# A graph network on one core: the first convolution as a slot layer

## The chip, the cores and the metric

The kernel runs on one core of one Trainium2 chip. The metric is the device time of one execution in microseconds (us). The kernel before takes 2701.87 us (median of 3 runs, 2697.64 to 2702.93).

## What is computed

A graph has 3125 nodes with 128 features and 53125 edges, each with a source, a target, one of 8 types and 16 attributes. Four networks follow one another; each adds its result to x and normalizes:

```python
h = relu(x @ proj + b)                       # network 0, two rounds
for l in range(2):
    msgs = trans[edge_type, src]             # trans = h times edge_W[l][t], t of 8
    agg = segment_sum(msgs, dst)
    h = relu(gru_cell(agg, h))
x = layernorm(x + h @ out_w + out_b)
# network 1: three rounds of the same form, with messages divided by the count
# of their (type, target), root weights, a bias and a residual
# network 2: one aggregation to the source node, scaled by degrees
# network 3: mean of the edge attributes by target and by source, then an MLP
```

A network's sum over edges is called a convolution here. Network 0 has two of them, network 1 three, network 2 one.

## The kernel before

**Start (lines 517 to 536, 1042, 808, 1253, 1532).** SyncE loads biases, weights and x, then the edge lists. TensorE projects x to h in 7 chunks and multiplies each of 25 blocks of h by the 8 type weights. ScalarE and VectorE bring each product to `big`, SyncE writes it to a table `messages` in DRAM. VectorE's list arithmetic (`window_starts`, `rows`, `sender_blocks`) runs between these copies, then come `windows` and `edge_data`, which also write constants. The semaphore `zeros` says that these are done. SyncE then clears the attribute rows in DRAM and loads marks.

**First loop (`first_loop` on each engine).** The edges are taken in 52 groups of 8 tiles of 128. Per group, GpSimd gathers 8 tiles of messages from the table (line 694), TensorE adds them into the window of targets by one-hot products (834), VectorE adds that to `acc` (1590). This is the first convolution. The loop also builds what the later layers need: ranks of the edges within blocks of source nodes (TensorE 817 and 818, VectorE's `ranks`, line 1561 first), counts by target and type (842), and the placing of every edge's payload in a slot (ScalarE 1274, 1280, 1285, TensorE 848, adding into one PSUM bank). TensorE's order is: rank product of group g+1, then messages, counts and slots of group g. Marks (the edge attributes) have four buffers; SyncE reloads one when ScalarE has copied it (`attr_kept`).

**After the loop.** VectorE turns the bank into slot lists (`slots`, lines 1739 to 1759), counts cells (`count_cells`, to 1777) and places them (`place_cells`, 1781 to 1806), beside the first recurrent unit (`gru(0, i)`, 7 chunks; line 1993 is VectorE's first step in a chunk). Its state product (line 926) has run before the loop.

**Slot layers.** Every other convolution of networks 0 and 1 is one. A *tile* (125 of them): VectorE compares a list of slots with the lane number (`shot`, line 1902), TensorE spreads the rows of a source block over the slots (956), ScalarE copies the result to `xs` (1302), SyncE stores 256 KB of records in `chunks`. Tiles come in 5 rounds of 25. A *window* (149): GpSimd gathers 128 records of 2 KB by an index list (`rec`, line 694, 6 buffers), VectorE builds four one-hots of target and type (`dhot`, 1923), TensorE sums (984). After each 12 windows a *transform* multiplies the sums by the 8 type weights (969). `plan(k)` orders tiles and windows. Layer 1, the second convolution, does all tiles and then all windows; in layers 2, 3 and 4 (network 1) windows follow their tiles by a round and the layers run into one another (`joined`). A window may be gathered when the last tile of its round is stored.

In layer 1, GpSimd also puts a target code beside each record (751), and VectorE beside the tiles inverts the counts (from tile 20), judges flags (tile 60) and makes the index list in six pieces (`list_piece`, lines 1827 to 1835, from tile 66 on). `list_piece` needs two lists that SyncE stores and loads back (656, 658).

**Edge attributes.** GpSimd scatters every tile of them to a row by rank in DRAM (`send_attrs`, line 703, 416 scatters), for the last aggregation. They stand in GpSimd's order beside layer 1 (96), ahead of and beside layer 2 (128), beside layers 3 and 4 (88 each) and ahead of the last aggregation (16). Their marks are loaded again, into weight buffers that are free by then.

The order of all this is written out by hand: each engine runs its own list, and semaphores join them.

## Time and profile before

| What | us |
|---|---|
| Median of 3 runs | 2701.87 |
| The profiled execution | 2686.08 |
| Its span, first to last instruction | 2684.0 |
| TensorE busy in the span | 2390.2 |
| VectorE busy | 1844.6 |
| GpSimd busy | 1591.1 |
| ScalarE busy | 856.3 |
| Message table's products (lines 808, 809; 50 and 50) | 26.4 and 25.5 |
| Gathers of messages in the loop (416) | 400.0 |
| Gathers of records in layers 1 to 4 (596) | 589.4 |

The mean clock granted to TensorE was 0.964 of full speed. Busy time counts instructions at work; an engine that waits for a semaphore is idle. GpSimd's instructions for a transfer end before the transfer lands. A row of the timeline gives in brackets how long the engine was idle before it, and whose end it waited for.

### The profile page before, as it was taken

To read this page: it belongs to the slowest core of one execution; us is meant where nothing else is said; L and a number is where in the kernel's file an instruction comes from. 1 tells how busy PE (TensorE), PEld (TensorE's weight loads), DVE (VectorE), ACT (ScalarE), POOL (GpSimd) and SP (SyncE) were. 2 spreads that over 40 slices of the span, in tenths; PEclk is the share of its full clock that TensorE was granted. 3 is DMA by queue.
4 is the path that set the end of the run, shared out by engine and by line. 5 is a ranking of instruction groups with operands and counts; after the bars stand their busy time and mean duration, and the time that the engine had idled before them with its cause. 6 is when DMAs were issued, how large, how long until landed. Compare 5 with 4: busy or idle time off the path is not lost.

```text
span 2684.0 us, 45747 instructions
## 1 busy us (share of the span) xinstructions
PE 2390.2 (89%) x15645; PEld 2130.7 (79%) x15645; DVE 1844.6 (69%) x6137; ACT 856.3 (32%) x1498; POOL 1591.1 (59%) x1706
## 2 busy tenths in 40 slices
PE   7798888886877999879999989999899987987998
PEld 3587777773777998569999989999899985876896
DVE  4887777766775886687776588766567874443785
ACT  3476665652442111332222322212222210444002
POOL 0777777765566664755666367776377773677000
PEclk9899999998998999799999999999999997999999
DMA  8422222222997665179998799888899871677891
GB/s 299 125 65 63 61 63 62 63 51 92 252 253 212 181 172 147 32 225 280 281 276 257 249 294 287 260 265 253 276 282 271 261 203 39 213 261 240 262 268 55
DMA packets 271661, 520.15 MB, mean 194 GB/s; under 512 B 62015, under 2 KB 115698, under 8 KB 270645
## 3 DMA queue, kind: packets, MB, share of 16 engines
q1 hardware_dynamic: 185197, 289.49, 34.9%
q0 software_dynamic: 86224, 227.59, 29.3%
q8 instruction: 134, 2.20, 0.3%
q14 instruction: 106, 0.87, 0.1%
HBM read 323.93 MB, written 192.99 MB: 193 GB/s over the span
## 4 chain that ended last, share of the span: by engine, by line
PE 50%; POOL 20%; DMA 12%; issue 8%; DVE 7%; ACT 2%; DVEq 0%; SPq 0%; POOLq 0%; ACTq 0%
PE ps L984 21%; POOL msg L694 15%; PE ps L956 9%; PE ps L969 6%; PE ps L1199 5%; DMA rec<-chunks,idx 4%; DMA chunks<-xs 3%; DMA chunks<-xo,put_idx 2%; POOL chunks L792 2%; POOL rec L694 2%; DVE shot L1902 1%; PE ps L1174 1%; POOL attributes L703 1%; PE ps L1018 1%; DMA srow<-lanes_of_slots 1%
## 5 line engine op out<-in xcount | busy, mean ns | idle before, releaser
L694 POOL DMA_INDIRECT rec<-chunks,idx x596 | 589.4, 989 | 366.8 <-PE ps L984 142.6
L984 PE MATMUL ps<-dhot,rec 128*128 128x168 f32 x4768 | 739.4, 310 | 52.2 <-DMA rec<-chunks,idx 29.7
L984 PEld LDWEIGHTS ps<-dhot,rec 128*128 128x128 f32 x4768 | 694.8, 192 | 71.1 <-DVE dhot L1923 37.3
L1923 DVE TENSOR_SCALAR dhot<-iota,dcode 128x168 f32<-128x168 f32 x2384 | 589.1, 311 | 93.7 <-PE ps L984 85.5
L956 PE MATMUL ps<-hrow,shot 126*128 126x128 f32 x4000 | 498.7, 279 | 51.5 <-DVE shot L1902 39.6
L956 PEld LDWEIGHTS ps<-hrow,shot 126*128 126x128 f32 x4000 | 477.9, 194 | 64.0 <-issue 32.4
L694 POOL DMA_INDIRECT msg<-messages,idx_buf x416 | 400.0, 962 | 195.7 <-issue 195.4
L1302 ACT ACTIVATE xs<-ps 128x512 f32<-128x512 f32 x500 | 296.8, 597 | 668.4 <-PE ps L956 604.9
L703 POOL DMA_INDIRECT attributes<-w,rank_to x368 | 373.9, 1016 | 178.9 <-issue 119.1
L1902 DVE TENSOR_SCALAR shot<-srow,lane_no 126x512 f32<-126x512 uint8 x500 | 232.3, 490 | 89.7 <-DMA srow<-lanes_of_slots 50.1
L848 PE MATMUL ps<-big,lane1h 128*128 128x300 f32 x832 | 224.0, 423 | 0.7 <-ACT big L1285 0.7
L1965 DVE TENSOR_TENSOR agg_rows<-ps,tmp 128x504 f32<-128x504 f32 (+1 forms) x150 | 101.4, 676 | 157.0 <-PE ps L984 155.2
L848 PEld LDWEIGHTS ps<-big,lane1h 128*128 128x128 f32 x832 | 153.9, 190 | 55.4 <-issue 9.1
L792 POOL DMA_INDIRECT chunks<-xo,put_idx x149 | 147.1, 987 | 82.2 <-ACT xo L1409 49.2
L1280 ACT ACTIVATE tmp<-iota,slot_col 128x300 f32<-128x300 f32 x416 | 186.3, 530 | 10.5 <-DVE slot_col L1574 10.4
L1174 PE MATMUL ps<-yrows,thot 126*128 126x128 f32 (+1 forms) x1192 | 150.8, 285 | 31.3 <-ACT xo L1409 28.6
L969 PE MATMUL ps<-agg_rows,w 128*128 128x252 f32 (+1 forms) x832 | 178.6, 368 | 0.0
L1174 PEld LDWEIGHTS ps<-yrows,thot 126*128 126x128 f32 (+1 forms) x1192 | 142.6, 198 | 38.8 <-ACT xo L1409 35.5
L969 PEld LDWEIGHTS ps<-agg_rows,w 128*128 128x128 f32 x832 | 151.4, 190 | 15.1
L2118 DVE TENSOR_SCALAR thot<-trow,lane_no 126x512 f32<-126x512 uint8 x149 | 79.1, 532 | 109.3 <-PE ps L1174 108.7
L834 PE MATMUL ps<-onehot,msg 128*128 128x128 f32 x832 | 105.2, 280 | 52.9 <-DMA msg<-messages,idx_buf 52.9
L834 PEld LDWEIGHTS ps<-onehot,msg 128*128 128x128 f32 x832 | 98.6, 193 | 64.3 <-issue 64.3
(289 smaller groups left out, 2495.6 us busy)
## 6 DMA issues: line engine op xcount, KB each, us to landing
chunks<-xs SPq DMA_DIRECT2D x375, 256.0 KB
tmp<-inverse_counts SPq DMA_DIRECT2D x36, 1008.0 KB, 10.3
chunks<-xs SPq DMA_DIRECT2D x125, 258.0 KB
srow<-lanes_of_slots SPq DMA_DIRECT2D x100, 320.0 KB, 5.7
grec<-chunks SPq DMA_DIRECT2D x125, 256.0 KB
messages<-big SPq DMA_DIRECT2D x25, 504.0 KB
trow<-lanes_of_targets SPq DMA_DIRECT2D x30, 320.0 KB, 4.1
rec<-chunks,idx POOLq DMA_INDIRECT x596, 5.0
```

The source lines that it names most:

```text
L694: eng.indirect_dma_start(buf, None, table, bass.IndirectOffsetOnAxis(ap=index, axis=0)).then_inc(sem, 16)
L703: eng.indirect_dma_start(attr_d, bass.IndirectOffsetOnAxis(ap=rank_to[:, c:c + 1], axis=0), attr_rows(k, n // G)[:, n % G * TC + T:(n % G ...
L792: eng.indirect_dma_start(x1_d, bass.IndirectOffsetOnAxis(ap=put_idx[:, v:v + 1], axis=0), xo[:, v % XO, :], None)\
L834: last = mm(ps[:, g % 2, 0:P], msg[:, g % SUB, t, :], onehot[:, g % 2, t, :], start=t == 0, stop=t == G - 1)
L848: last = mm(ps[:, 7, near_col(g):near_col(g) + NEAR], lane1h[:, g % 2, t, :], big[:, g % 2, t * NEAR:(t + 1) * NEAR], start=False, stop=Fa ...
L956: last = mm(ps[:, STAGE1_BANKS[i % 3], j * P:(j + 1) * P], shot[0:BS, i % SS, j * P:(j + 1) * P], hrow[0:BS, sb_, :], start=True, stop=True)
L969: last = mm(out, wt(REL[k], T)[:, t * P:(t + 1) * P], agg[gi % 2][:, t, 0:c1 - c0], start=t == 0, stop=k == 1 and t == T - 1)
L984: last = mm(ps[:, 4 + i % 2, (v % 3) * WT:(v % 3 + 1) * WT], rec[:, v % RS, j * P:(j + 1) * P], dhot[:, v % DS, j * WT:(j + 1) * WT], star ...
L1174: last = mm(ps[:, STAGE1_BANKS[v % 3], j * P:(j + 1) * P], thot[0:nodes_of(c), v % SS, j * P:(j + 1) * P], yrows[0:nodes_of(c), c, :], sta ...
L1302: act(xs[:, i % XS, 0:4 * P], ps[:, STAGE1_BANKS[i % 3], :], ACT.Copy).then_inc(q("x1_evac"), 1)
L1902: vec.tensor_scalar(shot[0:BS, i % SS, :], srow[0:BS, s_ % NS, (n % QS) * SPAN:(n % QS + 1) * SPAN], lane_no1[0:BS], None, ALU.is_equal).t ...
L1923: last = vec.tensor_scalar(dhot[:, v % DS, j * WT:(j + 1) * WT], iota[:, 0:WT], dcode[:, v, j:j + 1], None, ALU.is_equal)
```

## The change

The first convolution leaves the loop: the message table, its stores, the gathers, the message products and the additions to `acc` go. It becomes slot layer 1. The former layers 1 to 4 become 2 to 5. Layers 1 and 2 are woven by the same `plan`: windows follow their tiles by a round, transforms between them.

The edge lists are loaded first, and the list arithmetic runs at once. The record rows in DRAM are cleared in 50 transfers during the loop. The first state product stands within layer 1, at tiles 64 to 100, on ScalarE's copies. `slots`, `count_cells` and `place_cells` stand before layer 1. In layer 1 the flags are judged at tile 5, the six list pieces come at tiles 8 to 18 and the inverse counts at tiles 26 to 50. ScalarE puts the target codes, not GpSimd.

The scatters of attributes are divided anew. Those of the 26 even groups go out in the loop, from the marks that are there; GpSimd computes their rows itself (nine small operations per group). Those of the 26 odd groups go out beside layers 1 and 2, 104 in each, 0.7 behind each window's gather. Layers 3 to 5 and the last aggregation have none.

```diff
-AT = {1: range(0, 12), 2: range(12, 28), 3: range(28, 39), 4: range(39, 50), 5: range(50, 52)}
...
+AT = {1: range(0, LATE_GROUPS // 2), 2: range(LATE_GROUPS // 2, LATE_GROUPS)}
...
+CLEARS = 50
+LISTED, INVERTED, STATES = 22, 56, range(64, 106, 6)
...
-                at.append((NQ + v if k == 1 else when, 1, "sums", v))
+                at.append((when, 1, "sums", v))
...
+        def woven(k):
+
+            for kind, n in plan(k):
+                yield kind, n
+                if kind == "sums" and n % GW == 4 and n >= GW:
+                    yield "transform", n // GW - 1
+            yield "transform", NGRP - 1
...
+            def first_layer():
+                for kind, i in woven(1):
+                    if kind != "tile":
+                        continue
+                    store_tile(1, i)
+                    if i == LISTED:
+                        eng.wait_ge(q("idx_ready"), PIECES)
+                        attr_load(1)
+                    if i == INVERTED:
+                        eng.wait_ge(q("inv_ready"), INV_PIECES)
+                        eng.dma_start(inv_d, res[TYPE_ROWS, 0:NU]).then_inc(q("inv_stored"), 16)
...
+                for s in range(NS - 1):
+                    lanes_load(2, s)
+                after(eng, "gru_h", 0, NCH)
+                attr_load(2)
...
-            table_stores(0, flat)
...
+            for g in range(NG):
+                eng.wait_ge(q("attr_kept"), g + 1)
+                if g % 2 == 0 and g >= SUB:
+                    marks_sent(eng, g - SUB)
+                eng.dma_start(mark[:, g % SUB, :], mark_d[:, ds(g * (G * TC), G * TC)])\
+                   .then_inc(q(f"mark_loaded_{g % SUB}"), 16)
+                if g < CLEARS:
+                    n = RECS // CLEARS
+                    eng.dma_start(x1_d[g * n:(g + 1) * n, :].rearrange("(p r) c -> p r c", r=5),
+                                  no_rows[0:n // 5].unsqueeze(1).to_broadcast([n // 5, 5, RECORD_COLS]))\
+                       .then_inc(q("records_cleared"), 16)
...
-            attr_load(attrs_0, AT[1][:6])
-            attr_load(attrs_2, AT[1][6:])
+            eng.wait_ge(q("rows_cleared"), 32)
+            eng.wait_ge(q("lanes_stored"), 16)
+            for s in range(NS - 1):
+                lanes_load(1, s)
...
-            layer(1)
+            eng.wait_ge(q("records_cleared"), 16 * CLEARS)
+            first_layer()
+            second_layer()
...
+            def rows_of_ranks(g):
+
+                tiles = slice(g * G, (g + 1) * G)
+                eng.wait_ge(q("slot_known"), g + 1)
+                st.did(eng.tensor_scalar(sent[:, 0, :], rank_f[:, tiles], float(CAP), 1e6, ALU.is_ge, ALU.mult))
+                st.did(eng.tensor_scalar(sent[:, 1, :], src_sb[:, tiles], float(CAP), None, ALU.mult))
+                st.settle()
+                st.do(eng.tensor_tensor(sent[:, 1, :], sent[:, 1, :], sent[:, 0, :], ALU.add))
+                st.do(eng.tensor_tensor(sent[:, 1, :], sent[:, 1, :], rank_f[:, tiles], ALU.add))
+                st.did(eng.tensor_scalar(sent[:, 0, :], sent[:, 1, :], float(RANKS), None, ALU.is_ge))
+                st.did(eng.tensor_tensor(sent[:, 2, :], own_row[:, tiles], sent[:, 1, :], ALU.subtract))
+                st.settle()
+                st.do(eng.tensor_tensor(sent[:, 2, :], sent[:, 2, :], sent[:, 0, :], ALU.mult))
+                st.do(eng.tensor_tensor(sent[:, 1, :], sent[:, 1, :], sent[:, 2, :], ALU.add))
+                st.do(eng.tensor_copy(rank_to[:, tiles], sent[:, 1, :]))
...
+            def send_marks(g):
+
+                s = g % SUB
+                eng.wait_ge(q(f"mark_loaded_{s}"), 16 * (g // SUB + 1))
+                for t in range(G):
+                    c = g * G + t
+                    eng.indirect_dma_start(attr_d, bass.IndirectOffsetOnAxis(ap=rank_to[:, c:c + 1], axis=0),
+                                           mark[:, s, t * TC + T:(t + 1) * TC], None).then_inc(q(f"mark_sent_{s}"), 16)
...
-            eng.wait_ge(q("code_ready"), 1)
-            eng.wait_ge(q("rows_cleared"), 32)
-            for n in range(AT_FIRST[1]):
-                send_attrs(1, n)
-            for i in range(NQ):
-                if i >= XS:
-                    slot_wait(eng, "x1_stored", XS, 1, NQ, i - XS)
...
-                if i % 2 == 0:
...
+            rows_of_ranks(0)
+            for g in range(0, NG, 2):
+                if g + 2 < NG:
+                    rows_of_ranks(g + 2)
+                send_marks(g)
             eng.wait_ge(q("idx_ready"), PIECES)
...
                     rows_of(rec[:, v % RS, :], x1_d[0:RECS + 1, :], idx[:, v:v + 1], q(f"rec_got_{v % RS}"))
-                    if k == 2 and v % 3 == 1 and AT_FIRST[k] + v // 3 < G * len(AT[k]):
-                        send_attrs(k, AT_FIRST[k] + v // 3)
-                    n = 2 * (v // 3 - 4) + v % 3 - 1
-                    if k >= 3 and v % 3 > 0 and 0 <= n < G * len(AT[k]):
-                        send_attrs(k, n)
...
+                    if k <= 2:
+                        n = G * len(AT[k])
+                        for i in range(v * n // NW, (v + 1) * n // NW):
+                            send_attrs(k, i)
...
+            def first_state(c):
+
+                if c >= 1:
+                    after(eng, "state_kept", 0, c)
+                mm(bank(3, c), wt("whh0_n"), chunk(h, c), start=True, stop=True).then_inc(q("state_mm"), 1)
...
             def first_layer():
-                for i in range(NQ):
-                    spread_slots(1, i)
-                for v in range(NW):
-                    sum_window(1, v)
-                    if v % GW == 4 and v >= GW:
-                        transform(1, v // GW - 1)
-                transform(1, NGRP - 1)
+                for kind, n in woven(1):
+                    if kind == "tile":
+                        if n in STATES:
+                            first_state(STATES.index(n))
+                        spread_slots(1, n)
+                    elif kind == "sums":
+                        sum_window(1, n)
+                    else:
+                        transform(1, n)
...
-            candidate_state(0)
             eng.wait_ge(q("far_known"), 1)
+            after(eng, "h_ready", 0, NCH)
             first_loop()
...
             eng.wait_ge(q("loop_done"), 1)
+            eng.wait_ge(q("loaded_rest"), 2 * 16)
+            for c in range(NCH):
+                turn_rows(1, c)
+            eng.wait_ge(q("src1_ready"), 1)
+            for j in range(4):
+                last = mm(ps[0:NQ, 7, j * P:(j + 1) * P], src1[:, j * NQ:(j + 1) * NQ], wt("ident"), start=True, stop=True)
+            last.then_inc(q("lanes_mm"), 1)
+            eng.wait_ge(q("lanes_ready"), 1)
+            eng.wait_ge(q("cells_known"), 1)
+            mm(ps[0:TB, 7, 0:NWP], wb("before", TB, TB), cells, start=True, stop=True).then_inc(q("starts_mm"), 1)
+            first_layer()
...
+                    turn_rows(2, i - 1)
...
-            candidate_state(1)
-            first_layer()
+            second_state()
+            second_layer()
...
+            def first_state(c):
+
+                if c == 0:
+                    eng.wait_ge(q("inv_stored"), 16)
+                after(eng, "state_mm", 0, c + 1)
+                act(chunk(res, c), bank(3, c), ACT.Copy).then_inc(q("state_kept"), 1)
...
             first_loop()
+            for c in range(NCH):
+                keep_rows(1, c)
+            layer(1)
+            attrs_sent(eng, 1)
             for i in range(NCH + 1):
                 gru(0, i)
                 if i >= 1:
-                    keep_rows(1, i - 1)
-            layer(1)
+                    keep_rows(2, i - 1)
+            layer(2)
+            attrs_sent(eng, 2)
...
+                st.do(vec.tensor_tensor(to, rank, own, ALU.min))
+                eng.wait_ge(q("pool_steps"), RANK_STEPS * (NG // 2))
...
                 eng.wait_ge(q("placed"), NG + 1)
+                eng.wait_ge(q("records_cleared"), 16 * CLEARS)
...
-                beside = {1: [(20 + 4 * a, invert_counts, a) for a in range(INV_PIECES)] + [(60, judge)]
-                             + [(66 + 4 * a, list_piece, a) for a in range(PIECES)]}.get(k, [])
+                beside = {1: [(5, judge)] + [(8 + 2 * a, list_piece, a) for a in range(PIECES)]
+                             + [(26 + 4 * a, invert_counts, a) for a in range(INV_PIECES)]}.get(k, [])
...
-            for c, beside in enumerate([window_starts, None, rows, None, sender_blocks] + [None] * (NCH - 5)):
-                table(0, c, flat)
-                if beside:
-                    beside()
+            window_starts()
+            rows()
+            sender_blocks()
             windows()
             edge_data()
-            keep_state(0)
...
             rank_rows()
             slots()
             count_cells()
+            place_cells()
+            layer(1)
             for i in range(NCH):
                 gru(0, i)
-                if i == 2:
-                    place_cells()
             keep_state(1)
-            layer(1)
+            layer(2)
```

## Rows read from the trace of the kernel before

**Rows 1.** The profile's page, parts 1 and 5: engines, and TensorE's message products.
```profile
PE 2390.2 (89%) x15645; PEld 2130.7 (79%) x15645; DVE 1844.6 (69%) x6137; ACT 856.3 (32%) x1498; POOL 1591.1 (59%) x1706
...
L834 PE MATMUL ps<-onehot,msg 128*128 128x128 f32 x832 | 105.2, 280 | 52.9 <-DMA msg<-messages,idx_buf 52.9
```

**Rows 2.** Timeline of one loop period: start us, us, engine line op, operands, [idle before <-releaser].
```profile
343.51 0.36 DVE L1561 TENSOR_TENSOR rank_prod<-sb1h,ps 128x200 f32<-128x200 f32 x1 [2.21 <-PE ps L818]
...
347.43 3.58 ACT L1280 ACTIVATE tmp<-iota,slot_col 128x300 f32<-128x300 f32 x8
...
348.68 0.94 POOL L694 DMA_INDIRECT msg<-messages,idx_buf  x1 [0.30 <-issue]
...
348.90 4.31 PE L848 MATMUL ps<-big,lane1h 128*128 128x300 f32 x16
...
351.05 2.30 ACT L1285 ACTIVATE big<-tmp,w 128x2400 f32<-128x2400 f32 x1
...
353.92 0.36 DVE L1561 TENSOR_TENSOR rank_prod<-sb1h,ps 128x200 f32<-128x200 f32 x1 [2.21 <-PE ps L818]
```

**Rows 3.** Windows, third layer: us, PE PEld DVE ACT POOL busy (x), clock, DMA, GB/s.
```profile
1660.00:1760.00 100.00, 97.22 (x696) 94.55 (x695) 72.05 (x242) 20.40 (x35) 76.57 (x77) 1.00 0.90 268
```

**Rows 4.** Timeline around the second recurrent unit and the next layer's start.
```profile
1067.35 1.11 PE L917 MATMUL ps<-acc,w 128*128 128x504 f32 x2 [1.48 <-issue]
...
1150.90 3.59 PE L956 MATMUL ps<-hrow,shot 126*128 126x128 f32 x24 [1.15 <-DVE shot L1902]
...
1194.56 1.11 POOL L694 DMA_INDIRECT rec<-chunks,idx  x1 [17.69 <-DMA chunks<-xs]
```

**Rows 5.** Timeline of the start: VectorE's last constant, ScalarE's first marks.
```profile
79.42 0.15 DVE L1501 TENSOR_SCALAR lane_no<-lane_no 128x1 f32<-128x1 f32 x1
...
96.96 0.31 ACT L1274 ACTIVATE marks<-mark 128x128 f32<-128x128 f32 x1 [16.55 <-DMA mark<-in_marks]
```

**Rows 6.** Groups by line: busy us, mean ns | idle before; the addition into acc.
```profile
L1590 DVE TENSOR_TENSOR acc<-acc,ps 128x128 f32 x52 | 14.4, 276 | 8.7 <-PE ps L834 8.7
```

**Rows 7.** Instructions on the tile code: duration ns min/median/max, first and last start.
```profile
L751 POOL COPY xs<-code x125: 176/193/857, 662.8 to 827.7; 128x4 f32<-128x4 f32 x125
```

**Rows 8.** Chain of waits (start us, us, what): the last attribute scatter's landing.
```profile
829.31 3.59 DMA attributes<-rec,rank_to
```

**Rows 9.** Transfers by issuing line: count, size, median us from issue to landing.
```profile
mark<-in_marks SPq DMA_DIRECT2D x52, 96.0 KB, 2.0
...
agg_rows<-lists SPq DMA_DIRECT2D x1, 1950.0 KB, 9.2
tmp<-lists SPq DMA_DIRECT2D x1, 1875.0 KB, 6.9
```

**Rows 10.** Timeline from the loop's last product to the end of the placing of cells.
```profile
602.67 4.31 PE L848 MATMUL ps<-big,lane1h 128*128 128x300 f32 x16
...
618.74 0.30 DVE L1777 TENSOR_TENSOR dhot<-dhot 25x150 f32<-25x150 f32 x1
...
638.77 0.30 DVE L1781 COPY dhot<-ps 25x150 f32<-25x150 f32 x1 [1.83 <-PE ps L1080]
...
642.33 0.72 DVE L1993 SCALAR_TENSOR_TENSOR tmp<-res,bias,tmp 128x504 f32<-128x504 f32 x1
```

**Rows 11.** Chain of waits: tiles (8 matmuls each), a transform (16), windows (8 each).
```profile
674.02 3.82 PE ps L956 x32
...
1265.65 3.40 PE ps L969 x16
1273.29 3.42 PE ps L984 x24
```

**Rows 12.** Timeline of VectorE: the starts of two pieces of the list.
```profile
754.71 0.55 DVE L1827 TENSOR_SCALAR dhot<-agg_rows,lane_no 128x650 f32<-128x650 f32 x1
...
761.14 0.55 DVE L1827 TENSOR_SCALAR dhot<-agg_rows,lane_no 128x650 f32<-128x650 f32 x1
```

**Rows 13.** Waits of TensorE in the fourth layer: us in total, times, longest us.
```profile
PE ps L984 <- DMA rec<-chunks,idx: 15.8, 14, 3.9
```

More of the change, by code:

```diff
@@ L43 @@
 PASSES = NG // SUB
-AHEAD = 3
 NONE = 8191
@@ L606, in layer @@
                         inv_load(i // GW + 1)
[L607 to L608 removed]
+                after(eng, "acc_evac", 5, NGRP)
+                for j in (3, 4, 5):
                     general(j)
@@ L761, in _ @@
+            for k in range(1, 6):
                 for v in range(NW):
-                    if k == 1 and v == 0:
-                        for i in range(NQ - XS, NQ):
-                            slot_wait(eng, "x1_stored", XS, k, NQ, i)
-                    if k >= 2 and v in (0,) + LIMITS:
+                    if v in (0,) + LIMITS:
                         done = TB * (((0,) + LIMITS).index(v) + 1)
-                        done = ROUND_0 if k >= 3 and v == 0 else done
+                        done = ROUND_0 if k >= 4 and v == 0 else done
@@ L969, in transform @@
                     last = mm(out, wt(REL[k], T)[:, t * P:(t + 1) * P], agg[gi % 2][:, t, 0:c1 - c0], start=t == 0,
-                              stop=k == 1 and t == T - 1)
-                if k >= 2:
-                    last = mm(out, wt(f"root{k - 2}"), feed(k)[:, c0:c1], start=False, stop=True)
+                              stop=k <= 2 and t == T - 1)
+                if k >= 3:
+                    last = mm(out, wt(f"root{k - 3}"), feed(k)[:, c0:c1], start=False, stop=True)
                 last.then_inc(q("xf_mm"), 1)
@@ L1336, in layer @@
                             keep_rows(j, n)
-                for j in (1,) if k == 1 else (2, 3, 4):
+                for j in (3, 4, 5) if k == 3 else (k,):
                     with bad(eng):
@@ L1951, in layer @@
                         update(j, n)
-                after(eng, "acc_evac", 4, NGRP)
-                for j in (2, 3, 4):
+                after(eng, "acc_evac", 5, NGRP)
+                for j in (3, 4, 5):
                     general(j)
```

505 lines of the change are left out of this document (208 added, 297 removed).

## The prediction

> **What bounds the kernel now.** I read the busy shares first, then the stages, then one period of the long loop, then the queue of GpSimd.
>
> TensorE is busy 2390 of 2684 us [rows 1], so 294 us of idling is all that a better order could win while its work stays. The first loop does not run at TensorE's pace. One of its 52 groups takes 353.92 - 343.51 = 10.4 us, and the row that closes it shows VectorE waiting 2.2 us for TensorE [rows 2]. TensorE is late because GpSimd issues one gather per 0.94 + 0.30 = 1.24 us, so 8 gathers take 9.9 us: GpSimd sets the pace. From the layers on, TensorE is nearly full: 97.2 of 100 us in the stretch of [rows 3], with GpSimd at 77 instructions in the same 100 us, one per 1.30 us. That is GpSimd's ceiling as well: 76.57 us of busy time over 77 is 0.99 each, and with the 0.30 us of issue that stands between any two [rows 2] the queue is full.
>
> **The change, part by part.** I build the new timeline from the span's start and compare it with that of before at one point: the first tile of the third aggregation (the second of before), at 1150.90 us [rows 4].
>
> *Start.* The table of messages and the first state product go, the list loads come first. Before, VectorE finishes its constants at 79.4 us and ScalarE's first copy of marks starts 17.5 us later, at 97.0, behind the clearing of the attribute rows in the DMA queue [rows 5]. Now VectorE starts as its lists land (near 8 us; about 1.1 MB), does the same lane arithmetic (about 25 us in all), and waits once for the projections, since the flag product stands behind them in TensorE's order. I put the constants at 38 us (33 if the projections are early, 42 if late) and ScalarE's start at 55.5, with 50 and 60 as bounds.
>
> *The loop.* 416 gathers, 832 matmuls and 52 additions leave it; 26 groups of 8 scatters come in, each led by nine small GpSimd operations, and 50 transfers that clear records. GpSimd then has (8 x 1.30 + nine operations) per two groups, about 14 us, and is no longer full. Two things can be late next. VectorE: its part of a period is 10.4 - 2.2 = 8.2 us, less the 0.28 us addition that goes [rows 6]; that leaves 7.9 at most, and about 7.4 if some half a microsecond of small waits within it goes too. And a new ring: the marks of an even group are reloaded only when GpSimd has sent the group four before, and it sends that one only after it has the ranks of the group two before. I walk once round. Nine small operations: the nearest row is GpSimd's copy of codes, 0.19 us at the median and 0.86 at most [rows 7]; with a wait behind most of them I take 3.5 us for the nine (2 to 8). Eight scatters: 7 x 1.30, and 3.6 from the last one's start to its landing [rows 8], 12.7. The reload of marks: 2.0 [rows 9], and 0.2 for SyncE. ScalarE: a copy of 0.3 [rows 5], then 351.05 + 2.30 - 347.43 = 5.9. TensorE's slot product and the rank product behind it, to VectorE's start: 353.92 - 348.90 = 5.0. VectorE to the next rank: between 2 and 3.9 (its start at 343.51 to ScalarE's at 347.43, which holds a wait); I take 2, since the ten operations there are short. Sum 31.6 us, and it spans four groups: 7.9 each. With the ring and VectorE this close I take 8.0 (7.4 to 9.1). SyncE stands in that wait too; behind it are the record clearings and the odd group's marks, which have several us to spare. The clearings (0.66 MB each, some 3 us) are hidden by a DMA system that has little else there.
>
> So the last slot product ends at 55.5 + 10 (the first group's way) + 51 x 8.0 = 473.5. Before, it ends at 602.67 + 4.31 = 607.0 [rows 10]. That is 133.5 us won.
>
> *Between loop and layer.* Before, the slot lists, the counts and the placing of cells run beside the first recurrent unit. Now the first tile waits for them. From 607.0 to the last count operation is 12.1 us, the placing is 642.33 - 638.77 = 3.6, the counting product between them about 0.6, and the first comparison and tile 1.3. I take 17.5; the transposes of the first chunks lie beside it. First tile at 491.
>
> *First convolution as a layer.* TensorE's work for it is new: per tile 3.82 / 4 = 0.955 us, per window 1.14, per transform 3.40 [rows 11], so 125, 149 and 13 of them are 119 + 170 + 44 = 333 us. But what ends last is GpSimd. Its 149 gathers and 104 scatters at 1.30 are 329 us, and none of it can start before the 25 tiles of the first round are stored and the list of chunks is there. That start is late here. The list loads take 9.2 and 6.9 us [rows 9] and are asked for once the placing is done, so they land some 18 us behind the first tile; VectorE comes to the first piece at tile 8 and stands there, with all shots behind it, and TensorE behind them. Six pieces follow at 6.4 us with four shots between [rows 12], so about 5.6 with two: 33 us. Then the tiles up to the 24th and their landing, and the load of attributes in the same queue. I take 63 us from the first tile to the first gather (55 to 75). To the end: 148 windows of 253 x 1.30 / 149 = 2.21 us are 327, then landing, one-hots, window, transform and evacuation, 13. Sum 403. The state products (7 x about 0.9) lie in TensorE's slack: 100 tiles, 149 windows and 13 transforms are 309 us or 2.08 per window, against GpSimd's 2.21; the inverse counts and codes lie in VectorE's.
>
> *First recurrent unit.* Before, 674.02 - 607.0 = 67 us from loop end to first tile. Its first VectorE step waited for the lists and counts (about 6 of their 12.1 us; the gates' products take the rest) and later for the placing (3.6): 57 without them.
>
> *Second convolution.* The same plan without lists. The like layer of before needs 1194.56 - 1150.90 = 43.7 us to its first gather, with a reduction beside each tile that these layers lack; I take 39. Then 327 + 13. Sum 379. Before, the layer took 1067.35 - 674.02 = 393 [rows 4, 11]: first all tiles, then all windows. The weaving wins 14 us and not the 50 that TensorE's work would allow, because the scatters put GpSimd in its place.
>
> *The rest.* The next two layers to carry scatters lose them. In the last of them TensorE waits 15.8 us for records [rows 13], and those waits are where scatters and a load of marks hold gathers up. I count 20 us for all three (5 to 35). The 16 scatters ahead of the last aggregation lie beside normalization and give nothing.
>
> **The sum.** First tile of the third aggregation: 491 + 403 + 57 + 379, and 83.5 for the second recurrent unit and its normalization (1150.90 - 1067.35), is 1413.5. That is 262.6 later than 1150.9; less 20, 243. The profiled execution took 2686.1 us (span 2684.0), so 2929 on its scale; the median of the three runs is 2701.9, 0.6% more, so I forecast 2945.
>
> In short, the way from loop end to that tile grows from 544 to 940 us, by 396, and the 416 gathers that go give back 133.5, since VectorE needs the loop for 7.4 us or more of each 10 anyway.
>
> **Rivals.**
> *1. TensorE's pace in the two new layers.* If gathers run far enough ahead, a window costs 2.08 or less instead of 2.21 and the tail is short: about 25 us less in each, 2895. Against it: in [rows 3] a lighter load (five instructions per three windows, 2.17 us) already keeps GpSimd full. For it: TensorE still reaches 97% there. 0.13.
> *2. A slow ring.* VectorE and GpSimd hold each other up, and the nine operations take 8 us instead of 3.5: 36 us round, 9.1 each, 57 us more, 3002. The codes' copy, four elements wide, goes from 0.19 to 0.86 us beside a VectorE less busy than in the loop [rows 7]. 0.2.
> The Trainium skill (SBUF — State Buffer, "SBUF: two separate sides") has a rule for it: VectorE with two inputs in SBUF, or in a two-port mode, and a GpSimd operation lock one port pair, each for its whole instruction. The trace agrees for the small copies by their 0.86 us; the gathers' 0.94 beside a busy VectorE show little of it.
> *3. Not slower.* TensorE's idling is all lack of gathered data, and the new order fills it. Its own work rises by 333 and falls by 105, the message products [rows 1], and by some 50 for the table: about 178 more. So it decides in favour if the 294 us of idling fall to 116 or less, to 4% of the span; at 116 it gives the 2702 of before. Against it: VectorE alone holds the loop to 7.4 us a group, and about 50 us of gaps are new (17.5 ahead of the layer, and of its first 63 us what 25 tiles of 0.955 leave over). 0.02.
> My forecast, with its own range of 2905 to 2980: 0.65.
>
> **How the numbers follow.** The likeliest case gives 2945. The range takes in its bounds (loop at 7.4: -31; a start 10 us off; 63 as 75) and most of rivals 1 and 2: 2882 to 3010. About 0.2% is what a measurement here can tell from no change. Slower 0.98, same 0.01, faster 0.01.
>
> **What would show it.** Right: a loop of 8 us per group with GpSimd idle in it; a gap of 17 to 18 us without tiles behind it; VectorE waiting near the eighth tile for the lists; and in the two new layers TensorE waiting for gathered records, with GpSimd at 77 instructions per 100 us. Wrong: a loop period over 8.5 (the ring), GpSimd waiting for windows in those layers (rival 1), or the transfers of records as the longest wait, which I left out because the new layers load no inverse counts.

## The result: 2916 us, 7.96% slower

The changed kernel takes 2916.47 us (median of 4 runs, 2911.35 to 2919.85) where the kernel before took 2701.94 beside it: a ratio of 1.0796, 95% interval 1.0775 to 1.0816. The forecast was 2945 with a range of 2882 to 3010. The profiled execution took 2914.79 us, its span is 2912.9. A second set on another chip gave 2910.17 against 2686.76, 1.0823 [1.0783, 1.0862].

The profile's page after the change, parts 1 and 5 (engine or line, busy us, share or mean ns, count | idle before):

```profile
PE 2603.8 (89%) x17138; PEld 2359.5 (81%) x17138; DVE 2007.9 (69%) x6771; ACT 954.4 (33%) x1748; POOL 1376.2 (47%) x1548
...
L854 PE MATMUL ps<-big,lane1h 128*128 128x300 f32 x832 | 241.6, 447 | 39.0 <-ACT big L1283 38.7
```

TensorE is busy 214 us longer [rows 1] and its idle time is 309 us instead of 294. So of the added 229 us, 214 are, in sum, work added to TensorE and 15 are more idling: the added work found no gap to lie in. Where it sits is seen in the stages. First the timeline (start us, us, engine line op, operands, idle before and its releaser), answering [rows 4, 5, 10, 11]:

```profile
33.96 0.44 DVE L1514 TENSOR_SCALAR own_row<-iota,lane_row 128x416 f32<-128x416 f32 x1
...
50.14 0.31 ACT L1272 ACTIVATE marks<-rec 128x128 f32<-128x128 f32 x1 [27.49 <-DMA rec<-in_marks]
...
463.50 4.31 PE L854 MATMUL ps<-big,lane1h 128*128 128x300 f32 x16
...
484.99 5.19 PE L964 MATMUL ps<-hrow,shot 126*128 126x128 f32 x24 [4.20 <-DVE shot L1906]
...
499.07 0.56 DVE L1831 TENSOR_SCALAR dhot<-agg_rows,lane_no 128x650 f32<-128x650 f32 x1 [6.18 <-DMA tmp<-lists]
...
904.27 0.26 ACT L1316 ACTIVATE acc<-ps 128x105 f32<-128x105 f32 x1 [1.39 <-PE ps L977]
...
964.76 1.46 PE L964 MATMUL ps<-hrow,shot 126*128 126x128 f32 x11 [1.24 <-DVE shot L1906]
...
1421.58 0.68 PE L964 MATMUL ps<-hrow,shot 126*128 126x128 f32 x4 [1.10 <-DVE shot L1906]
```

They are, in order: constants ready, first marks, last slot product, first tile of layer 1, VectorE at the first list piece, last evacuation of layer 1, first tile of layer 2, first tile of the third aggregation. Then GpSimd's first and last gather of records in layers 1, 2 and 5:

```profile
550.27 0.99 POOL L714 DMA_INDIRECT rec<-chunks,idx  x1 [79.19 <-DMA chunks<-xs]
...
891.50 0.96 POOL L714 DMA_INDIRECT rec<-chunks,idx  x1 [0.30 <-issue]
...
999.12 0.96 POOL L714 DMA_INDIRECT rec<-chunks,idx  x1 [105.34 <-DMA chunks<-xs]
...
1326.98 0.96 POOL L714 DMA_INDIRECT rec<-chunks,idx  x1 [0.30 <-PE ps L992]
...
2155.94 0.94 POOL L714 DMA_INDIRECT rec<-chunks,idx  x1 [31.37 <-DMA chunks<-xs]
...
2449.45 0.94 POOL L714 DMA_INDIRECT rec<-chunks,idx  x1 [0.30 <-issue]
```

And the same two rows for the last layer of the kernel before, which still sent 88 scatters there:

```profile
1899.88 0.94 POOL L694 DMA_INDIRECT rec<-chunks,idx  x1 [31.55 <-DMA chunks<-xs]
...
2218.77 0.98 POOL L694 DMA_INDIRECT rec<-chunks,idx  x1 [0.30 <-PE ps L984]
```

Against the forecast, stage by stage, in us:

| Stage | Forecast | Measured |
|---|---|---|
| ScalarE's first marks | 55.5 | 50.1 |
| First marks to end of the last slot product | 418.0 | 417.7 |
| Loop end to first tile | 17.5 | 17.2 |
| First tile to first gather, layer 1 | 63 | 65.3 |
| First to last gather, layer 1 | 327 | 341.2 |
| Last gather to last evacuation | 13 | 13.0 |
| To the first tile of layer 2 | 57 | 60.2 |
| First tile to first gather, layer 2 | 39 | 34.4 |
| First to last gather, layer 2 | 327 | 327.9 |
| Last gather to first tile of the third aggregation | 96.5 | 94.6 |
| From there to the end, against 1533.1 before | -20 | -41.7 |

The first tile of the third aggregation comes at 1421.6 (forecast 1413.5), 270.7 us later than before [rows 4]; 41.7 are given back behind it, which leaves 228.9.

### The profile page after: what moved, and what is told of

Same layout as the page of the kernel before. It is cut to its first block, busy times and chain, and to the rows that moved or that the text cites. A ratio compares the mean times of both kernels' runs of the same rounds, so it can differ in the third digit from the quotient of the medians.

```text
span 2912.9 us, 49789 instructions
## 1 busy us (share of the span) xinstructions
PE 2603.8 (89%) x17138; PEld 2359.5 (81%) x17138; DVE 2007.9 (69%) x6771; ACT 954.4 (33%) x1748; POOL 1376.2 (47%) x1548
## 4 chain that ended last, share of the span: by engine, by line
PE 57%; DMA 14%; POOL 10%; DVE 10%; issue 5%; ACT 4%; SPq 0%; DVEq 0%; POOLq 0%; ACTq 0%
PE ps L992 23%; PE ps L964 13%; PE ps L977 6%; DMA rec<-chunks,idx 5%; PE ps L1208 4%; DMA chunks<-xo,put_idx 3%; POOL rec L714 3%; DMA chunks<-xs 2%; POOL attributes L747 2%; PE ps L854 2%; POOL attributes L722 2%; POOL chunks L805 2%; ACT tmp L1278 1%; DMA rec<-in_marks 1%; DVE lane1h L1592 1%
## 5 line engine op out<-in xcount | busy, mean ns | idle before, releaser
L714 POOL DMA_INDIRECT rec<-chunks,idx x745 | 738.1, 991 | 966.8 <-PE ps L992 432.2
L992 PE MATMUL ps<-dhot,rec 128*128 128x168 f32 x5960 | 930.0, 310 | 69.3 <-DMA rec<-chunks,idx 35.9
L992 PEld LDWEIGHTS ps<-dhot,rec 128*128 128x128 f32 x5960 | 873.3, 192 | 88.6 <-DVE dhot L1927 40.6
L1927 DVE TENSOR_SCALAR dhot<-iota,dcode 128x168 f32<-128x168 f32 x2980 | 732.1, 310 | 192.6 <-PE ps L992 184.5
L964 PE MATMUL ps<-hrow,shot 126*128 126x128 f32 x5000 | 630.8, 280 | 55.8 <-DVE shot L1906 37.8
L964 PEld LDWEIGHTS ps<-hrow,shot 126*128 126x128 f32 x5000 | 607.0, 196 | 70.1 <-issue 36.0
L854 PE MATMUL ps<-big,lane1h 128*128 128x300 f32 x832 | 241.6, 447 | 39.0 <-ACT big L1283 38.7
L747 POOL DMA_INDIRECT attributes<-rec,rank_to x208 | 216.7, 1042 | 64.9 <-issue 57.5
L722 POOL DMA_INDIRECT attributes<-tmp,rank_to x208 | 211.0, 1015 | 63.4 <-issue 63.1
L1208 PE MATMUL ps<-grec,ghot 128*126 128x144 f32 x1000 | 130.8, 290 | 12.9 <-DMA grec<-attributes 12.8
L1208 PEld LDWEIGHTS ps<-grec,ghot 128*126 128x126 f32 x1000 | 125.2, 190 | 18.2 <-issue 18.2
```

The costliest lines, as they stand in the source:

```text
L714: eng.indirect_dma_start(buf, None, table, bass.IndirectOffsetOnAxis(ap=index, axis=0)).then_inc(sem, 16)
L722: eng.indirect_dma_start(attr_d, bass.IndirectOffsetOnAxis(ap=rank_to[:, g * G + n % G:g * G + n % G + 1], axis=0), tmp_flat[:, at + T:at ...
L747: eng.indirect_dma_start(attr_d, bass.IndirectOffsetOnAxis(ap=rank_to[:, c:c + 1], axis=0), mark[:, s, t * TC + T:(t + 1) * TC], None).the ...
L854: last = mm(ps[:, 7, near_col(g):near_col(g) + NEAR], lane1h[:, g % 2, t, :], big[:, g % 2, t * NEAR:(t + 1) * NEAR], start=False, stop=Fa ...
L964: last = mm(ps[:, STAGE1_BANKS[i % 3], j * P:(j + 1) * P], shot[0:BS, i % SS, j * P:(j + 1) * P], hrow[0:BS, sb_, :], start=True, stop=True)
L992: last = mm(ps[:, 4 + i % 2, (v % 3) * WT:(v % 3 + 1) * WT], rec[:, v % RS, j * P:(j + 1) * P], dhot[:, v % DS, j * WT:(j + 1) * WT], star ...
```

## The experiments

Four kernels ran on one chip, four on a second and four on a third; each experiment below says on which. The changed kernel itself ran beside them on the second alone (the 2910.17 us above). The first chip differs: the kernel before took 3034.47 us there (14 runs, 3008.15 to 3045.43), but 2686.76 and 2687.89 on the other two. Times of the first set are compared only with each other; those of the second and third also across.

### What holds the two new layers: scatters left out

```diff
                     rows_of(rec[:, v % RS, :], x1_d[0:RECS + 1, :], idx[:, v:v + 1], q(f"rec_got_{v % RS}"))
-                    if k <= 2:
-                        n = G * len(AT[k])
-                        for i in range(v * n // NW, (v + 1) * n // NW):
-                            send_attrs(k, i)
```

> The changed kernel without the 208 scatters that GpSimd sends beside the windows of its first two layers; the attributes of every second group are left out of the sums. The profile of the changed kernel has 341.2 us from the first to the last gather of layer 1 and 327.9 in layer 2, with 253 GpSimd instructions in each, at 1.30 us. Theory (GpSimd sets the pace of these layers): TensorE's own work is left, some 310 us from the first gather to the layer's end where 354 and 338 are now, so 35 to 60 us less in all, about 2870 (45 less), and GpSimd then waits for windows at most gathers. Rival (TensorE's pace already, GpSimd only looks full): 10 us less at most, 2906 or more.

It took 2904.38 us on the first chip. The kernel with eight mark buffers, which differs only in the loop, took 3069.86. That is 165 us, too much to carry over, so it ran again on the third chip:

> The changed kernel without the 208 scatters beside its first two layers, again (the attributes of every second group are missing from the sums), with the changed kernel's own level known here as 2910. On the other chip the two layers took 308 and 297 us from first to last gather without scatters; the woven first layer of the kernel before took 304 with 20. Theory (GpSimd sets the pace of the changed kernel's 341 and 328): 60 to 70 us less, 2845. Rival (most of the gap on the other chip was that chip's slow scatters, and here TensorE sets the pace): 20 us less or nothing, 2890 or more.

It took 2829.32 us (2823.93 to 2841.29), 81 less than the changed kernel's 2910.17. Its first and last gathers of layers 1 and 2, and what GpSimd waited for in layer 1 (us in total, times, longest):

```profile
541.00 0.99 POOL L713 DMA_INDIRECT rec<-chunks,idx  x1 [80.63 <-DMA chunks<-xs]
...
849.05 0.95 POOL L713 DMA_INDIRECT rec<-chunks,idx  x1 [0.30 <-issue]
...
952.88 1.98 POOL L713 DMA_INDIRECT rec<-chunks,idx  x1 [102.88 <-DMA chunks<-xs]
...
1246.47 1.01 POOL L713 DMA_INDIRECT rec<-chunks,idx  x1 [0.30 <-issue]
```

```profile
POOL rec L713 <- PE ps L987: 126.4, 58, 4.4
```

In the changed kernel the same waits of GpSimd in the same stretch are these:

```profile
POOL rec L714 <- DMA chunks<-xs: 85.6, 3, 79.2
POOL rec L714 <- issue: 34.8, 114, 0.3
POOL attributes L722 <- issue: 31.7, 104, 0.3
POOL rec L714 <- PE ps L992: 17.5, 32, 2.4
```

Without scatters GpSimd waits for windows, 126.4 us in 58 waits. With them it waits 17.5, and as the 0.30 us between two instructions are counted in each of the 32 waits, only some 8 of that are real waiting. The rest of its gaps, but for one wait of 6.13 us for a store, are those 0.30 us. The gathers take 308.1 us instead of 341.2 and 293.6 instead of 327.9, so GpSimd's queue costs 33 and 34 us. That is 67 of the 81. The two profiles differ by 91 us; of the 24 beyond the 67, 14 lie behind the last record gather of the last layer (460.8 us against 475.2), a part that differs by 12 between two profiles of the changed kernel itself, and 6.5 in the first loop, which is the same in both kernels; the rest comes in steps of up to 4 us, some of them the other way. I read no effect of the scatters from them.

### What holds the loop: buffers, scatters, small operations

```diff
+MB = 8
...
-        mark = rec_flat[:, 0:SUB * WIDE].rearrange("p (s c) -> p s c", s=SUB)
+        mark = rec_flat[:, 0:MB * WIDE].rearrange("p (s c) -> p s c", s=MB)
...
-                    marks_sent(eng, g - SUB)
+                    marks_sent(eng, g - MB)
```

> The changed kernel with eight buffers for the marks instead of four: the same work, but a buffer is reloaded only eight groups after it was filled, so the way round GpSimd, the reload, ScalarE, TensorE and VectorE spans eight groups. Theory (this ring sets the 8.0 us per group): the period falls to what VectorE needs, 7.6 us as between its starts at 305.38 and 313.01, 20 us less, 2896, and ScalarE's waits for loaded marks (107 us in 25) all but vanish. Rival (VectorE is the pace, held up by GpSimd's operations beside it): no change, 2916.

> The changed kernel whose loop sends nothing: the 208 scatters of even groups and the nine small GpSimd operations ahead of each eight are left out, so their attributes are missing from the sums. Neither the ring nor GpSimd is in the loop. Theory (ring alone costs time): the loop runs at VectorE's 7.6 us per group, 20 us less, 2896, within 5 us of the kernel with eight buffers. Rival (VectorE and GpSimd lock each other out): VectorE's operations get shorter as well, 7.2 us per group or less, 2875, and the kernel with eight buffers stays behind it by 15 us or more.

On the first chip the eight buffers took 3069.86 us and the loop that sends nothing 3026.43. VectorE's 52 rank steps ran there from 36.2 to 466.3 and from 38.3 to 428.7, 8.43 and 7.65 us apart on average. ScalarE no longer waited for marks, and yet most second groups still took about 9.5 us instead of 7.5. That spoke for the rival. The third chip said otherwise:

> The eight mark buffers again, since the first look was on a chip where the kernel before took 3034 us and where VectorE stood 2 us at every second group whatever the buffers. On a chip with the kernel before near 2690: in the changed kernel VectorE's starts are 7.5 us apart with a longer one, 9.4 to 12 us, at every fourth to sixth group, 8.13 on average. Theory (the ring through the marks' reload makes those): they go, the average is 7.7 (with the second start at 17 us as everywhere), 22 us less than the changed kernel's 2910, 2888. Rival (the scatters themselves hold the other engines up, as they seem to on the other chip): the longer ones stay, 8.1 or more, 2905 or more.

> The loop without its 208 scatters and the small GpSimd operations ahead of them, again (their attributes are missing from the sums). It had exactly 7.5 us at each of the 49 later groups on the other chip. Both theories have that again: 22 us less than the changed kernel, 2888; what counts is the distance to the eight buffers: none, if the ring is all; 15 us or more, if the scatters hold the engines up.

> The changed kernel with the nine small GpSimd operations per even group kept and only the 208 scatters of the loop left out (their attributes are missing from the sums). If the small operations slow VectorE down (both working in SBUF), its starts are further apart than 7.5 us and its operations longer than in the loop that sends nothing; theory: no more than 3 us in all, 2888 to 2891. Rival: 0.3 us or more per group, 2903 or more.

Here is VectorE's rank step in the changed kernel, with eight buffers, without anything sent, and with the small operations alone, in this order, one row of each trace (duration ns min/median/max, first and last start):

```profile
L1572 DVE TENSOR_TENSOR rank_prod<-sb1h,ps x52: 357/364/365, 38.1 to 453.0; 128x200 f32<-128x200 f32 x52
```

```profile
L1574 DVE TENSOR_TENSOR rank_prod<-sb1h,ps x52: 358/363/365, 37.5 to 431.6; 128x200 f32<-128x200 f32 x52
```

```profile
L1560 DVE TENSOR_TENSOR rank_prod<-sb1h,ps x52: 361/363/365, 37.5 to 425.9; 128x200 f32<-128x200 f32 x52
```

```profile
L1564 DVE TENSOR_TENSOR rank_prod<-sb1h,ps x52: 354/363/365, 37.9 to 430.8; 128x200 f32<-128x200 f32 x52
```

Divided by 51 they give 8.14, 7.73, 7.62 and 7.70 us. The medians are 2910.17, 2891.84, 2886.22 and 2894.50 (2880.17 to 2903.96, the widest). So eight buffers bring 18 us; taking all sends away brings 24, hardly more; and the small operations alone cost nothing that can be told apart. The ring is the cause on this chip. Its price is less sure: 2910.17 is from the second chip. A loop with four buffers ran on the third as well, in the kernel without layer scatters:

```profile
L1567 DVE TENSOR_TENSOR rank_prod<-sb1h,ps x52: 357/364/365, 38.2 to 441.8; 128x200 f32<-128x200 f32 x52
```

That is 7.91 us a group, and from the first marks to the end of the last slot product it took 409.0 us where eight buffers took 396.0 and the changed kernel 417.7. On one and the same chip the eight buffers are thus worth 13 us in these profiles, not the 22 that the changed kernel's own profile gives. One round of the ring is seen in the changed kernel's timeline, where the marks' load holds ScalarE, and TensorE behind it holds VectorE:

```profile
305.38 0.36 DVE L1572 TENSOR_TENSOR rank_prod<-sb1h,ps 128x200 f32<-128x200 f32 x1 [2.43 <-PE ps L831]
...
307.42 0.28 POOL L729 TENSOR_SCALAR sent<-rank_f 128x8 f32<-128x8 f32 x1 [2.23 <-DVE slot_col L1585]
...
308.36 0.31 ACT L1272 ACTIVATE marks<-rec 128x128 f32<-128x128 f32 x1 [3.64 <-DMA rec<-in_marks]
...
310.71 1.06 POOL L747 DMA_INDIRECT attributes<-rec,rank_to  x1 [0.28 <-POOL rank_to L739]
...
313.01 0.36 DVE L1572 TENSOR_TENSOR rank_prod<-sb1h,ps 128x200 f32<-128x200 f32 x1
```

VectorE stands 2.43 us and the next group takes 7.6. In the waits of the loop's stretch from 100 to 440 us this row heads the list of the changed kernel, and there is none like it with eight buffers:

```profile
ACT marks L1272 <- DMA rec<-in_marks: 67.7, 21, 4.6
```

How these waits become time is seen in TensorE's clock. Most groups of the changed kernel take 7.5 to 7.9 us; what lifts the average to 8.0 are seven groups of 9.4 to 12.0 us. In each of the seven the granted clock falls to half, from the level of 2.4 GHz to that of 1.2, after TensorE has waited 1.9 to 3.1 us for ScalarE's `big`. The slot product behind the wait, 4.31 us at full clock, then takes 5.9 to 7.3, as in this row:

```profile
104.73 7.34 PE L854 MATMUL ps<-big,lane1h 128*128 128x300 f32 x16 [2.75 <-ACT big L1283]
```

And this is the loop from 60 to 430 us in the changed kernel and with eight buffers (us, PE PEld DVE ACT POOL busy, granted clock, DMA share, GB/s):

```profile
60.00:430.00 370.00, 333.63 (x1669) 257.32 (x1668) 333.77 (x1426) 280.98 (x461) 249.15 (x391) 0.96 0.44 95
```

```profile
60.00:430.00 370.00, 349.88 (x1770) 260.31 (x1769) 354.25 (x1513) 296.74 (x491) 263.16 (x418) 1.00 0.46 100
```

With eight buffers the clock stays full in this stretch, and no group after the second takes over 7.7 us. In the whole loop the changed kernel's slot products take 241.6 us where the kernel before had 224.0 and the eight buffers have 225.7, so some 16 of the 22 us stand in slot products at the lower clock. The four-buffer loop on the third chip has three such falls in this stretch instead of seven, and its slot products take 232.1. What makes their number differ stays open.

### Weaving undone in the second layer

```diff
-                at.append((when, 1, "sums", v))
+                at.append((NQ + v if k == 2 else when, 1, "sums", v))
...
+                for i in range(G * len(AT[2]) if k == 2 else 0):
+                    send_attrs(k, i)
...
-                    if k <= 2:
+                    if k == 1:
```

> The changed kernel with its second layer in the old order, all 125 tiles and then all 149 windows; its 104 scatters go ahead of the gathers, beside the tiles. Theory (weaving wins 21 us in a layer, as 372 us here stand against 393 in the kernel before): tiles at the 1.27 us of their stores take 159 us, windows 221, the end 13, so 21 us more, 2937. Rival (weaving wins nothing, because it puts the scatters into GpSimd's queue at the windows): 2916 or less.

It took 3137.48 us on the first chip, 68 more than the eight buffers there, whose loop takes as long (last rank step at 464.8 and 466.3). This doesn't price the weaving, for something else broke in: while GpSimd sent 104 scatters in a row, some tiles took 22 us each. TensorE's tiles and SyncE's stores of five of them:

```profile
1098.29 2.07 PE L966 MATMUL ps<-hrow,shot 126*128 126x128 f32 x8 [20.33 <-issue]
1120.73 2.05 PE L966 MATMUL ps<-hrow,shot 126*128 126x128 f32 x8 [20.37 <-issue]
```

```profile
1054.84 88.55 SPq L565 DMA_DIRECT2D chunks<-xs  x5
```

The first gather came 163 us after the first tile (1191.79 less 1028.50) instead of 34. The experiment is inconclusive for what it was meant to ask.

### The parts of the change on the kernel before

Is it the weaving and the placing of scatters that helps, and the leaving of the loop that costs? Three kernels start from the kernel before, and their loop still gathers messages. All three ran on the second chip, beside its 2686.76 us.

```diff
-AT = {1: range(0, 12), 2: range(12, 28), 3: range(28, 39), 4: range(39, 50), 5: range(50, 52)}
-AT_FIRST = {1: 32, 2: 80, 3: 40, 4: 40}
+AT = {1: range(0, 12), 2: range(12, 30), 3: range(30, 40), 4: range(40, 47), 5: range(47, 52)}
+AT_FIRST = {1: 32, 2: 92, 3: 40, 4: 40}
...
```

> The kernel before with the same 416 scatters placed otherwise: of the 52 groups 18 instead of 16 go with its second layer (92 instead of 80 of their scatters ahead of it), 10 instead of 11 with the third, 7 instead of 11 with the fourth, 5 instead of 2 ahead of the last aggregation, and within a layer they are spread evenly over its windows. Theory (GpSimd's 237 instructions at 1.30 us hold the fourth layer at 318.9 us from first to last gather, where the changed kernel, without scatters there, takes 293.5, and 310.2 against 322.6 in the third): 30 to 38 us less, 0.986 to 0.989 of the kernel before. Rival (those layers got shorter in the changed kernel for another reason, such as less DMA traffic): less than 8 us.

2658.24 against 2686.76 us, 0.9901 [0.9866, 0.9936], 28.5 us less. The last layer's first and last gather:

```profile
1885.42 0.97 POOL L694 DMA_INDIRECT rec<-chunks,idx  x1 [28.36 <-DMA chunks<-xs]
...
2186.10 0.95 POOL L694 DMA_INDIRECT rec<-chunks,idx  x1 [0.30 <-issue]
```

300.7 us instead of 318.9, and in the third 316.4 (1538.36 to 1854.78) instead of 322.6. The same scatters cost 24 us less in these two layers once some of them stand where GpSimd has room. The gain is just short of the theory's 30 to 38 and far from the rival's 8. So GpSimd's queue held these layers.

```diff
-                at.append((NQ + v if k == 1 else when, 1, "sums", v))
+                at.append((when, 1, "sums", v))
...
+                beside = {1: [(5, judge)] + [(8 + 2 * a, list_piece, a) for a in range(PIECES)]
+                             + [(26 + 4 * a, invert_counts, a) for a in range(INV_PIECES)]}.get(k, [])
...
```

> The kernel before, whose loop still gathers the first convolution's messages, with its first slot layer woven (tiles and windows mixed, the lists early, the 50 clearing transfers in the loop); 76 of that layer's 96 scatters go ahead of its first gather. Theory (what weaving is worth in this layer when the gathers stay in the loop): about 50 us to the first gather, 300 for the windows at TensorE's pace, 13 at the end, 363 instead of 393: 30 us less, 0.989. Rival (the early lists, the clearing beside the gathers of the loop, and the scatters eat it up): within 8 us of the kernel before.

2666.41 us, 0.9933 [0.9905, 0.9962], 20 less. The layer's first tile, first and last gather:

```profile
674.05 2.92 PE L969 MATMUL ps<-hrow,shot 126*128 126x128 f32 x24 [1.04 <-DVE shot L1924]
```

```profile
728.40 0.99 POOL L713 DMA_INDIRECT rec<-chunks,idx  x1 [3.34 <-DMA chunks<-xs]
...
1032.80 0.94 POOL L713 DMA_INDIRECT rec<-chunks,idx  x1 [0.30 <-issue]
```

54.4 us to the first gather (theory 50) and 304.4 for the gathers (300); the last one starts 21 us earlier than before (1054.26). The loop's last rank step is at 587.4 and was at 586.6, so 50 transfers of 0.66 MB beside it cost at most 1 us. Weaving is worth 20 us, not 30.

> Both edits together: the kernel before with its first slot layer woven and its scatters spread. The two act on different layers, so theory has the sum, 60 to 68 us less, 0.975 to 0.978 of the kernel before. Rival (both relieve the same thing, and the second brings nothing): the better of the two alone.

2642.74 us (2634.09 to 2646.49), 0.9839 [0.9806, 0.9872]: 44 less, under the 60 to 68 of the theory, and nearly the 48.9 that the two bring alone. Of all kernels here this is the fastest, 1.6% ahead of the kernel before, and it keeps the gathers in the loop.

## Why the prediction was right, and where it was off

**The core of it.** The forecast was that the way from loop end to that tile grows by 396 us and that the gathers give back 133.5. The way grew from 543.9 to 953.8 us, 410, and the loop ended 139.2 earlier. But not all of that came from the gathers: 46.8 us are the earlier start of ScalarE's marks (50.1 for 97.0), and 92.4 are the loop itself (417.7 for 510.0). What bounds the gain is VectorE's 7.5 us a group. Even the loop that sends nothing leaves the kernel at 2886.22, 1.0734 of the kernel before. So no repair of the ring or the sends can pay for a layer of 420 us.

**Start.** The constants came at 34 instead of 38, inside the bounds, and the first marks 5.4 us early.

**The loop.** The forecast of 8.0 per group was hit, as the stage's 417.7 us show, and its cause was the one named: a ring (31.6 us for four groups; 4 x 7.96 = 31.8 measured over the last 49), with VectorE's 7.5 close behind it. That the two sums agree so well is partly luck. No steady round of 31.8 us is seen: most groups keep VectorE's pace, and seven long ones, with TensorE at half clock, make up the average. The forecast had no term for the clock. On the third chip the same loop ran at 7.76 over its last 49 groups. The nine small operations took 3.0 us, from 307.42 to 310.43, and not 3.5.

**Gap and head of layer 1.** 17.2 and 65.3 us; VectorE did stand 6.18 us for the lists where the forecast had it stand.

**The two layers.** GpSimd as the pace is shown by leaving scatters out. In layer 2 a window took 2.215 us (forecast 2.21). In layer 1 it took 2.306, and here the step of 148 windows at 2.21 was 14 us short. GpSimd's own instructions took the same in both layers (251.2 and 251.1 us); its gaps beyond 0.30 us were 13.6 us in layer 1 and 0.3 in layer 2: some 8 in waits for windows, 5 of them in the first 60 us, and 5.8 in the one wait for a store. That the one-hots of this layer need the code in the record itself (VectorE waits 97.7 us for records there) may be why windows came late; this is argued, not shown.

**The step that failed** is the last: "I count 20 us for all three (5 to 35)". It was 41.7, beyond its bound. By first and last gathers layer 3 gained 0.8, layer 4 12.5 and layer 5 25.4 us. I had read one wait of TensorE, 15.8 us [rows 13]. The right reading was the one that the forecast made for the new layers: 237 instructions of 1.30 us are 308, and the last layer took 318.9, so GpSimd held it, and TensorE alone would need less (293.5). The 11 us between 308 and 318.9 are waits of GpSimd in the layer's first 30 us, the longest, 7.94, for the load of marks. Moving scatters out of these layers of the kernel before gave 24 us there, which shows the cause. The 21.7 us that were missed here and the 8.1 that the stages ahead took too long have opposite signs, and those 8.1 are themselves a sum of misses from -5.4 to +14.2. That the total came so close is to that extent luck. So the forecast was 14 us high on the profile's scale, and 29 in the median, where I had added 0.6% for the distance of median and profile that the changed kernel doesn't show (2916.47 against 2914.79).

**Rival 1** (TensorE's pace) fell. But its price was too small: without scatters a window takes 2.08 us in layer 1 and 1.98 in layer 2, so GpSimd costs 33 us in each, not 25.

**Rival 2** (slow ring, locked ports) fell, in part. The ring was there, not slow; its 36 us are also 9.0 a group and not 9.1. With the nine operations alone VectorE's copy of 25 elements took 184 ns, without them 189, and its one-hots 280 and 282. GpSimd paid instead. Its last operation, a cast, takes 519 ns in the changed kernel, where it meets VectorE's scan, an instruction with two inputs in SBUF. It takes 190 in the kernel with the ranks alone, where it comes after the scan (mean ns behind the comma):

```profile
L739 POOL CAST rank_to<-sent 128x8 int32<-128x8 f32 x12 | 6.2, 519 | 0.8
```

```profile
L734 POOL CAST rank_to<-sent 128x8 int32<-128x8 f32 x14 | 2.7, 190 | 0.9
```

The Trainium skill (SBUF — State Buffer, "SBUF: two separate sides") says of a VectorE instruction with two inputs in SBUF and a GpSimd one that reads SBUF that whichever starts first holds the shared pair of ports for its whole instruction. The 519 beside 190 ns agree with GpSimd as the one that waits; the scan takes 628 and 627 ns in the two, so VectorE loses nothing to the small operations. Beside scatters it does lose: its copy takes 280 ns on average in the changed kernel and 189 in the loop that sends nothing, and its one-hots 294 and 282. The copy's two rows, from 200 to 400 us:

```profile
L1551 DVE COPY sb1h<-sb_seen 128x25 f32<-128x25 f32 x25 | 7.0, 280 | 0.0
```

```profile
L1539 DVE COPY sb1h<-sb_seen 128x25 f32<-128x25 f32 x27 | 5.1, 189 | 0.0
```

In the changed kernel the 19 copies that meet a scatter take 361 ns on average and the 8 that meet nothing on GpSimd take 187. With eight one-hots a group this is some 0.2 us a group.

**Rival 3** (not slower) asked for TensorE's idling to fall to 116 us. It rose to 309. TensorE's own work rose by 214 us, where the rival's working had 178. One part of that is the price of a window, 1.14 us in the forecast: the page after the change has 930.0 us for the matmuls of 745 windows, 1.25 each. The 17.6 us of the slower clock in the loop are another.

## What to carry to other kernels

Before work leaves a loop, ask which engine is late next, and how soon: the gathers took 10 us of each period, and VectorE needed 7.5 of it anyway, so what was left to give back was a quarter of the period. When instructions move between stages, count the moved engine's queue against the others in every stage, those that lose work too. When a wait goes through a buffer's reload, double the buffers first: it is the cheapest trial, and here it made the loop 13 us shorter on one chip. And look at the granted clock where a period is longer than its neighbours: waits of 2 to 3 us made the product behind them 1.6 to 3 us longer.

## What the chips showed that I had not expected

One chip ran the kernel before in 3034 us, 12.9% over the 2687 of the others, and the trouble is tied to scatters. Without any in a stretch the chips agree: layer 1's gathers took 308.1 us on both, the loop that sends nothing 7.5 us a group on both. With 104 scatters beside the windows they took 385.3 there against 340 on the third chip, in the loop, with eight scatters per two groups, most second groups took 2 us more, and with 104 in a row some tiles took 22 us and SyncE needed 88.55 us for five stores, while beside 76 in a row on the second chip it stored each five tiles in 3.89 to 12.85 us. Behind the last record gather of the last layer, where GpSimd puts 149 blocks of rows to DRAM by index, all four kernels took 502 to 506 us on the first chip, and all others took 461 to 475. The pages from that chip put 5 to 9% of the chain to "another core or an unknown queue" (3% where the layers' scatters were left out); those from the other chips put none there. The mean clock granted to TensorE was lower too, 0.908 to 0.916 for the kernel before against 0.959 and more on the third chip; whether that is a cause or follows from TensorE's waits no run shows. What held the engines there stays open; the kernel before was not profiled on it.
